# Layer 2's selective scan: who adds and copies y, softplus on both halves at once, and GpSimd's share of the states

## The reference, cut to what matters

```
Delta = softplus(dt_proj(x_dbl[dt]) + dt_bias)        # per direction, channel, position
def step(h, inp):
    dA = jnp.exp(dt_l[..., None] * A)
    h = h * dA + (dt_l * u_l)[..., None] * B_l[:, :, None, :]
    y = jnp.einsum('bkdn,bkn->bkd', h, C_l)
ys = ys + Ds.reshape(1, K, d, 1) * xs                 # skip, then the sum over the four directions
```

## Time and profile before

| what | value |
| --- | --- |
| median of 3 runs | 42,425.57 us (42,410.13 to 42,440.21) |
| the profiled execution's own time | 42,416.64 us |
| its span | 42,414.8 us |
| VectorE busy | 34,737.8 us (82%) |
| GpSimd busy | 31,168.8 us (73%) |
| TensorE matmul busy | 30,144.3 us (71%) |
| ScalarE busy | 20,384.3 us (48%) |
| DMA, mean | 106 GB/s |

### The profile page before, as it was taken

How to read it: one execution, slowest core, us unless ns; L and a number is a source line. 1 busy time by engine, 2 the same in 40 slices (tenths; PEclk the granted TensorE clock), 3 DMA queues, 4 the chain that set the end, 5 groups by cost and what they waited for, 6 DMA issues and landing times. The chain is left out here.

```text
span 42414.8 us, 275743 instructions
## 1 busy us (share of the span) xinstructions
PE 30144.3 (71%) x63524; PEld 11806.2 (28%) x63524; DVE 34737.8 (82%) x35406; ACT 20384.3 (48%) x37797; POOL 31168.8 (73%) x14520
## 2 busy tenths in 40 slices
PE   6767767777777777777767777777777777777777
PEld 3232232322323223232232322323223232232322
DVE  7959779597795977959779597795977959779597
ACT  4535445354453544535445354453544535445354
POOL 6939769397693976939769397693976939769397
PEclk8888888888888888888888888888888888888888
DMA  3414234142241422414234142341423414234142
GB/s 105 151 37 152 84 105 152 37 152 85 103 152 36 152 84 104 152 36 152 84 105 151 38 152 84 105 151 37 152 84 105 151 37 152 84 105 151 37 152 84
DMA packets 1221654, 4486.01 MB, mean 106 GB/s; under 512 B 144528, under 2 KB 146072, under 8 KB 1211680
## 3 DMA queue, kind: packets, MB, share of 16 engines
q1 hardware_dynamic: 1219872, 4466.97, 30.4%
HBM read 4399.30 MB, written 67.11 MB: 105 GB/s over the span
## 5 line engine op out<-in xcount | busy, mean ns | idle before, releaser
L567 PE MATMUL PS<-WORK,CST 128*128 128x512 f32 x36096 | 20046.6, 699 | 8354.6 <-POOL WORK L483 7561.8
L472 POOL TENSOR_TENSOR WORK<-WORK,XN 128x1024 f32<-128x1024 f32 x8192 | 19246.1, 2381 | 1.3
L567 PEld LDWEIGHTS PS<-WORK,CST 128*128 128x128 f32 x36096 | 7593.5, 222 | 20499.9 <-POOL WORK L483 10379.6
L921 ACT ACTIVATE PS<-WORK,AN 128x512 f32<-128x512 f32 x16384 | 10604.8, 678 | 1806.7 <-DVE WORK L1446 1092.8
L1438 DVE TENSOR_TENSOR_SCAN PS<-PS,HST,WORK 128x512 f32<-128x512 f32 x8960 | 10972.5, 1271 | 45.5 <-ACT PS L921 32.1
L1438 DVE TENSOR_TENSOR_SCAN WORK<-PS,HST,WORK 128x512 f32<-128x512 f32 x5376 | 6583.7, 1267 | 0.0
L483 POOL TENSOR_TENSOR WORK<-WORK,CWIDE 128x1024 f32<-128x1024 f32 x2048 | 4859.8, 2373 | 136.2 <-issue 83.0
L530 POOL MEMSET XN<- 128x66 f32 x32 | 4.9, 153 | 5777.4 <-DVE SM L1288 5675.4
L921 ACT ACTIVATE WORK<-PS 128x512 f32<-128x512 f32 (+3 forms) x2752 | 1628.6, 598 | 5296.8 <-PE PS L567 4589.4
L1446 DVE TENSOR_TENSOR WORK<-PS,WORK 128x1024 f32<-128x1024 f32 x3072 | 3762.3, 1225 | 105.1
L921 ACT ACTIVATE HST<-PS 128x2 f32<-128x2 f32 x4480 | 748.9, 167 | 6154.6 <-DVE WORK L1446 6154.0
(11 more groups left out here) (158 smaller groups left out, 27665.1 us busy)
## 6 DMA issues: line engine op xcount, KB each, us to landing
XN<-xbc_rows SPq DMA_DIRECT2D x4096, 512.0 KB, 3.7
WORK<-xbc_rows SPq DMA_DIRECT2D x2048, 512.0 KB, 3.9
CWIDE<-xbc_rows SPq DMA_DIRECT2D x2048, 512.0 KB, 4.2
BIG<-in_spec_dram SPq DMA_DIRECT2D x32, 2048.0 KB, 14.7
X<-in_x_dram SPq DMA_DIRECT2D x16, 2048.0 KB, 8.7
xbc_rows<-WORK SPq DMA_DIRECT2D x512, 64.0 KB, 3.2
out_dram<-X SPq DMA_DIRECT2D x16, 2048.0 KB, 6.3
TAP<-in_cw_dram SPq DMA_DIRECT2D x1, 576.0 KB
```

The costliest lines, as they stand in the source:

```text
L472: nc.gpsimd.tensor_tensor(S.both(S.Q[u % 6]), S.both(S.DU[u // SN % 2]), S.wide(S.BW, u).unsqueeze(1).to_broadcast([P, 2, NT]), MUL).then_ ...
L567: return nc.tensor.matmul(o, w, r, start=start, stop=stop)
L921: return nc.scalar.activation(o, i, f, **k)
```

## The change

- The first product into banks 0 and 1 of a group is now the former y (through the unit matrix) or, in the first direction, u times a diagonal matrix SKIP of the summed D. So the PSUM sum is the new y, and `take_y` becomes a ScalarE copy of 1024 columns, placed at n = 0 behind `decays(u + 1)`.
- `softplus`, `log_small` and `sum_dt` work on both halves in one instruction each. The dt bias becomes a ninth row of the dt product, against a row of ones. Places: `rows` n = 1 and 2, `split` 3, `steps` 4 and 5, `softplus` 5 to 10, one part each, `log_small` 10, `sum_dt` 10; `make_du` stays at 12.
- `POOL_STATES` is now taken modulo 32: of 32 units GpSimd weighs 11 in place of 12, n = 1, 3, 5, 7, 9, 14 in even groups and n = 1, 4, 6, 8, 14 in odd ones.

The diff, without the unchanged lines and the declaration of DTB2:

```diff
@@ -23,7 +23,7 @@
...
 GROUPS = 32
-POOL_STATES = (1, 4, 6, 9, 12, 14)
+POOL_STATES = (1, 3, 5, 7, 9, 14, 17, 20, 22, 24, 30)
@@ -163,6 +163,7 @@
...
         CWIDE = sb("CWIDE", 2 * 2 * NT)
+        ROW2 = sb("ROW2", NT); SKIP = sb("SKIP", 2 * P)
         XBC = nc.dram_tensor("xbc_rows", (2, 2 * SN, NT), fp32, kind="Internal").ap()
@@ -223,10 +224,11 @@
...
                 s.DU = [take(w) for _ in range(2)]
-                s.LE = take(w)
-                s.TA, s.E, s.MK, s.R = (take(NT) for _ in range(4))
+                s.LE, s.E = (take(w) for _ in range(2))
+                s.R = ROW2
                 s.BW = [XN[:, w * i:w * (i + 1)] for i in range(4)]
                 s.CW = [take(w) for _ in range(2)] + [CWIDE[:, w * i:w * (i + 1)] for i in range(2)]
+                s.MK = take(w)
                 s.rows_ready = sample_sem("s2_rows_ready")
@@ -252,7 +254,7 @@
...
-                return u % SN in s.pool
+                return u % (2 * SN) in s.pool
@@ -416,6 +418,8 @@
...
                 e.dma_start(dst, src).then_inc(weights_in, 16)
+            e.dma_start(DTW2[32 + RANK:33 + RANK, :].rearrange("o (k p) -> o k p", p=P), d["dtb2"].rearrange("(o p) k -> o k p", o=1),
+                        allow_slow_non_contiguous=True).then_inc(weights_in, 16)
             e.wait_ge(zeroed, 4)
@@ -447,16 +451,16 @@
...
-                def sum_dt(g, h):
-                    e.wait_ge(S.dt_steps, 4 * g + 2 * h + 2)
-                    e.wait_ge(S.softplus, 12 * g + 6 * h + 6)
-                    dt = S.DT[g % 2][:, ch(h)]
-                    nc.gpsimd.tensor_tensor(dt, dt, S.LE[:, ch(h)], ADD).then_inc(S.dt_made, 1)
+                def sum_dt(g):
+                    e.wait_ge(S.dt_steps, 2 * g + 2)
+                    e.wait_ge(S.softplus, 6 * g + 6)
+                    dt = S.DT[g % 2]
+                    nc.gpsimd.tensor_tensor(dt, dt, S.LE, ADD).then_inc(S.dt_made, 1)
...
-                    e.wait_ge(S.dt_made, 2 * g + 2)
+                    e.wait_ge(S.dt_made, g + 1)
                     if g >= 2:
@@ -483,18 +487,15 @@
...
-                sum_dt(0, 0)
-                sum_dt(0, 1)
+                sum_dt(0)
                 make_du(0)
...
                     if g + 1 < KDIR * NCH:
-                        if n == 8:
-                            sum_dt(g + 1, 0)
-                        if n == 11:
-                            sum_dt(g + 1, 1)
+                        if n == 10:
+                            sum_dt(g + 1)
                         if n == 12:
@@ -720,7 +721,7 @@
...
                     if h == 0 and g:
-                        e.wait_ge(S.dt_steps, 4 * g)
+                        e.wait_ge(S.dt_steps, 2 * g)
                     k = g // NCH
@@ -730,7 +731,24 @@
...
                     at = P * (2 * (g // NCH) + h)
-                    mm(bank(7 - h), DTW2[32:32 + RANK, at:at + P], S.R[32:32 + RANK, :]).then_inc(S.dt_raw, 1)
+                    mm(bank(6 + h), DTW2[32:33 + RANK, at:at + P], S.R[32:33 + RANK, :]).then_inc(S.dt_raw, 1)
+                def sum_up(u):
+                    g, n = u // SN, u % SN
+                    if n == 0:
+                        if g:
+                            e.wait_ge(S.y_taken, g)
+                        for h in range(2):
+                            if g < NCH:
+                                w, r = SKIP[:, ch(h, P)], S.cols(BIG1, g)[:, h]
+                            else:
+                                w, r = EYE, S.cols(BIG2, g)[:, h]
+                            mm(S.like(bank(h), g)[:, 0], w, r, True, False)
+                    S.wait_weighed(e, u)
+                    for h in range(2):
+                        r = mm(bank(h), EYE, S.Q[u % 6][:, ch(h)], False, n == SN - 1)
+                    r.then_inc(S.summed, 1)
@@ -739,16 +757,11 @@
...
                     if g + 1 < KDIR * NCH:
-                        if n < 2:
-                            rows(g + 1, n)
-                        if n in (3, 4):
-                            steps(g + 1, n - 3)
-                    S.wait_weighed(e, u)
-                    if n == 0 and g:
-                        e.wait_ge(S.y_taken, g)
-                    for h in range(2):
-                        r = mm(bank(h), EYE, S.Q[u % 6][:, ch(h)], n == 0, n == SN - 1)
-                    r.then_inc(S.summed, 1)
+                        if n in (1, 2):
+                            rows(g + 1, n - 1)
+                        if n in (4, 5):
+                            steps(g + 1, n - 4)
+                    sum_up(u)
@@ -1029,6 +1042,8 @@
...
+                raw = PS[:, 6:8, :]
                 def split(g):
@@ -1037,37 +1052,35 @@
...
-                def softplus(g, h, part):
-                    at = 12 * g + 6 * h
-                    raw = bank(7 - h)
-                    bias = DTB2[:, 2 * (g // NCH) + h:2 * (g // NCH) + h + 1]
+                def softplus(g, part):
                     if part == 0:
-                        e.wait_ge(S.dt_raw, 2 * g + h + 1)
-                        if 2 * g + h:
-                            e.wait_ge(S.dt_steps, 2 * (2 * g + h))
-                        act(S.TA, raw, ACT.Abs, bias=bias).then_inc(S.softplus, 1)
-                        e.wait_ge(S.softplus, at + 1)
-                        act(S.E, S.TA, ACT.Exp, scale=-1.0).then_inc(S.softplus, 1)
+                        e.wait_ge(S.dt_raw, 2 * g + 2)
+                        if g:
+                            e.wait_ge(S.dt_made, g)
+                        act(S.both(S.LE), raw, ACT.Abs).then_inc(S.softplus, 1)
                     elif part == 1:
+                        e.wait_ge(S.softplus, 6 * g + 1)
+                        act(S.E, S.LE, ACT.Exp, scale=-1.0).then_inc(S.softplus, 1)
+                    elif part == 2:
                         if g >= 2:
...
                             e.wait_ge(S.du_ready, g - 1)
-                        act(S.DT[g % 2][:, ch(h)], raw, ACT.Relu, bias=bias).then_inc(S.softplus, 1)
-                        e.wait_ge(S.softplus, at + 2)
+                        act(S.both(S.DT[g % 2]), raw, ACT.Relu).then_inc(S.softplus, 1)
+                    elif part == 3:
+                        e.wait_ge(S.softplus, 6 * g + 2)
                         act(S.MK, S.E, ACT.Relu, bias=vec["edge"], scale=-1.0).then_inc(S.softplus, 1)
+                    elif part == 4:
+                        e.wait_ge(S.softplus, 6 * g + 3)
+                        act(raw, S.both(S.E), ACT.Square, bias=vec["series"], scale=3 ** -0.5).then_inc(S.softplus, 1)
                     else:
-                        e.wait_ge(S.softplus, at + 3)
-                        act(raw, S.E, ACT.Square, bias=vec["series"], scale=3 ** -0.5).then_inc(S.softplus, 1)
-                        if g:
-                            e.wait_ge(S.dt_made, 2 * g)
-                        act(S.LE[:, ch(h)], S.E, ACT.Ln, bias=vec["one"]).then_inc(S.softplus, 1)
+                        act(S.LE, S.E, ACT.Ln, bias=vec["one"]).then_inc(S.softplus, 1)
...
                     if n == 0:
-                        e.wait_ge(S.dt_made, 2 * (u // SN) + 2)
+                        e.wait_ge(S.dt_made, u // SN + 1)
                     if u >= 2:
@@ -1093,22 +1106,30 @@
...
+                def take_y(g):
+                    e.wait_ge(S.summed, SN * (g + 1))
+                    act(S.cols(BIG2, g), S.like(PS[:, 0:2, :].rearrange("p d l -> p (d l)"), g), ACT.Copy)\
+                        .then_inc(S.y_taken, 1)
                 split(0)
-                for h in range(2):
-                    for part in range(3):
-                        softplus(0, h, part)
+                for part in range(6):
+                    softplus(0, part)
                 decays(0)
...
                         decays(u + 1)
+                    if n == 0 and g:
+                        take_y(g - 1)
                     if g + 1 < KDIR * NCH:
-                        if n == 2:
+                        if n == 3:
                             split(g + 1)
-                        if 4 <= n < 10:
-                            softplus(g + 1, (n - 4) // 3, (n - 4) % 3)
+                        if 5 <= n < 11:
+                            softplus(g + 1, n - 5)
                     if S.of(u)[1] < NCH - 1:
                         carry(u)
+                take_y(KDIR * NCH - 1)
@@ -1396,31 +1417,14 @@
...
-                def log_small(g, h):
-                    raw = bank(7 - h)
-                    e.wait_ge(S.softplus, 12 * g + 6 * h + 6)
-                    V.scalar_tensor_tensor(raw, raw, 13.0 / 16, S.E, ADD, MUL).then_inc(S.dt_steps, 1)
-                    e.wait_ge(S.dt_steps, 4 * g + 2 * h + 1)
+                def log_small(g):
+                    raw = PS[:, 6:8, :]
+                    e.wait_ge(S.softplus, 6 * g + 6)
+                    V.scalar_tensor_tensor(raw, raw, 13.0 / 16, S.both(S.E), ADD, MUL).then_inc(S.dt_steps, 1)
+                    e.wait_ge(S.dt_steps, 2 * g + 1)
                     V.memset(SM[:, 12:13], 0.0)
```

(32 more changed lines are left out.)

6 lines of the change are left out of this document (3 added, 3 removed).

## The result

| | before | changed |
|---|---|---|
| median, us | 42,425.57 (42,410.13 to 42,440.21, 5 runs) | 45,634.91 (45,614.15 to 45,647.86, 5 runs) |
| span of the profiled execution, us | 42,414.8 | 45,639.4 |
| mean granted TensorE clock | 0.866 | 0.852 |

The ratio is 1.0756 (95% interval 1.0741 to 1.0771): 3,209 us slower. The prediction said 43,920, between 43,000 and 44,450. The direction was right, the size was wrong by more than half: 1,494 us over the median of before were foreseen.

A forecast was written before the change was run, and what follows sets the result against it. GpSimd was taken as the bound (55.48 and 56.43 us a group), VectorE 2.5% behind. Changes of mean 3.2 us x 480 periods, 1,536, and ends of -29 gave 1,507 on 42,417: 43,920 us, range 43,000 to 44,450.

The forecast's parts named there:

- By busy times alone the groups would shrink. But the queues are in order and the new positions make a chain.: Layer 2's scan: busy times give GpSimd 55.3 (even) and 53.0 us (odd) a group; queue order gives 57.2 and 57.75.
- The first rival: Copy, products and softplus slip into idle time and GpSimd alone decides: 41,670 us, chance 0.12.
- TensorE needs 3.70 us for the sums of states 14 and 15.: Start of a direction 0 group: after these sums the take of y starts at t = 3.9 us.
- Sum(3) waits for GpSimd's weigh(3), the seventh slot, 6q + 2.35 = 16.2.: Even group, direction 0: TensorE's sum(3) waits until t = 16.2 us, ending 18.05; q is a GpSimd slot, 2.305 us.
- GpSimd would be there after 11 drives and 5 weighings, 16q = 36.9: Even group, direction 0: GpSimd reaches the dt addition at t = 36.9 us; q is its slot, 2.305 us.
- The walk: Prediction's step-by-step timing of one group through the engine queues, t = 0 at the end of GpSimd's slot for weigh(14).
- Decays(7) ready at 24.05, the addition to dt at 38.75.: Even group, direction 0: ScalarE's decays of state 7 stall VectorE 2.7 us; GpSimd's dt addition starts at t = 38.75.
- GpSimd's predicted wait of 1.9 us at the addition: Even group, direction 0: GpSimd, ready at t = 36.9, waits 1.9 us until the dt addition starts at 38.75.
- second rival: No change: steps come in time, VectorE's fix still holds odd groups; within 0.1%, 42,420 us, chance 0.05.
- The third rival: Slower by less: the strided copy and products cost nothing, all directions lose 2.0 us a group; 43,350 us, chance 0.13.
- Edits at no cost.: Merged softplus, dt bias row, bias DMA, SKIP set-up and B and C row store: no period changes; set-up under 5 us.
- The state that GpSimd gave up is no gain while it waits: Odd group, direction 0: GpSimd is at the addition at 34.6 us and waits 4.7; period 57.75.

The follow-up runs named there:

- kernels 8: Changed kernel plus unread TensorE products before state 14, y copied at n = 1, steps at 3, rows at 0, former-y or skip pair at 6: 42,012.03 us (0.9906).
- experiment 1: Changed kernel plus ten products whose result nobody reads, issued by TensorE before the sum of state 14: 44,935.61 us (1.0597).
- Experiment 9: Changed kernel with ScalarE's carry ahead of the copy of y, split and softplus of the same n, y copied at n = 1: 45,136.36 us (1.0643).
- experiment 10: Changed kernel reordered: rows at n = 14, steps and split 0, y copy 1, softplus 2 to 7, fix 9, former-y pair 6: 41,935.04 us (0.9886).

## Why the direction was right and the size wrong

**"By busy times alone the groups would shrink. But the queues are in order and the new positions make a chain."** Right, and shown: kernels 8 and 10 keep every part of the change and are faster than before. No instruction's own time costs the 3,209 us; their order does. The first rival's 41,670 was within 0.7% of what a good order reaches.

**"TensorE needs 3.70 us for the sums of states 14 and 15."** This step failed: it took a duration from a trace in which TensorE was at full clock. The new list leaves 10 to 13 to VectorE, TensorE is idle for 5.4 to 7.9 us, and the eight products take 5.1 to 6.8 us (13 sets, 530 to 1,300 us). y is copied at t = 5.45 (544.88 to 550.33) in direction 0 and 6.8 in direction 1, not at 3.9. Its worth, by experiment 1, is 699 us: 1.5 us a group. That is less than half of the 1,715 us by which the forecast fell short; with the clock mended, 44,936 is still 1,016 above it.

**"Sum(3) waits for GpSimd's weigh(3), the seventh slot, 6q + 2.35 = 16.2."** This step failed too, and with it "GpSimd would be there after 11 drives and 5 weighings, 16q = 36.9". The walk let GpSimd run freely from slot to slot up to the addition. It named what is queued in ScalarE ahead of the decays, and even wrote carry(5) down, but never asked who waits for the carries. GpSimd's weighing of a state does. In the direction 1 group shown above weigh(3) starts at 1313.97, t = 20.8, and not 6q = 13.8; the sum of state 3 and both steps follow it, and Abs starts at t = 29.3 in place of 24.7. These links feed each other: late y, late carry and decays, late weighing, late sum, late steps, late softplus, late carry. Direction 1, where each link is longer, lost 4.2 us a group more than the walk had and direction 0 lost 2.4; with the clock mended (experiment 1) 2.3 and 0.6 of it are left. Experiment 9 shows the carries as the cause of GpSimd's waits, and also that taking the carries out alone gives back only 299 us, since the decays stand behind the same three waits. So the missing term is seen, and its worth alone is not: what the runs give is 699 us for the clock and, for issuing the steps ahead of sum(3), 1,509, in which the waits that the walk did have are included.

**Decays(7) ready at 24.05, the addition to dt at 38.75.** In the even group of direction 0 Abs starts at t = 23.6 (22.1 by the walk) and the addition at 41.0. The 1.5 us of Abs are those of the clock: in experiment 1 it starts at 22.3. GpSimd's predicted wait of 1.9 us at the addition is there as 1.22 + 2.73 before two weighings, none at the addition. The sign that the prediction had named for its second rival (a wait in odd groups only) was thus seen, and did not mean that rival: the waits of the even groups had moved.

**The strides.** The third rival, that they cost nothing, fell at once: 1.88 for the copy, 3.68 for the pair. In the order of experiment 10 groups take 54.6 us in direction 0 and 56.0 in direction 1, a distance of 1.4 us where before it was 0.95: most of these strides' time is hidden there.

**"Edits at no cost."** Merging softplus was taken as free. Its operations are; but both halves now wait for both steps, and its place is later. Together with its places this part cost 1,732 us, the most of the three.

**The state list.** "The state that GpSimd gave up is no gain while it waits" was right and too mild: alone on the kernel before it costs 431 us, because VectorE at 97% became the bound.

**The rule on ScalarE.** The Trainium skill, Perfetto Trace Analysis, section "Optimizing Scalar/DVE Operations", says that offloading some work to ScalarE may make sense when VectorE is saturated. This case has it both ways: the same move costs 1,044 us where carries and decays queue behind its wait, and gains 459 us where they do not.

## What to carry to other kernels

When an instruction that waits is moved into a queue, list everything behind it there, and for each of these who waits for it, until the list ends or comes back to where it began; if it comes back, the delay is paid more than once in a period. Issue what depends on nothing late (here rows, split and time steps) ahead of the wait, not behind. Judge a part of a change in an order that lets it work: three parts that cost 3,209 us in one order gained 492 in another, and 1.9% with the load between two engines set anew.
